# Layer 1 attention: the sixteen selection candidates of wide score tiles from four runs of eight

## The reference

```
scores = q k^T / 8, causal; key heads shared by groups of four query heads
threshold = the 64th largest score of the row
scores below the threshold = -1e30
out = softmax(scores) v, then the output projection
```

## Time and profile before

| | |
|---|---|
| median of 3 runs | 2331.82 us (2328.57 to 2334.2) |
| the profiled execution, its own time | 2331.76 us |
| its span | 2330.1 us |
| busy, share of the span | PE 81%, DVE 71%, ACT 60%, POOL 29% |
| layer 1 attention | about the last 1150 us |

### The profile page before, as it was taken

One profiled execution on the slowest core, in us unless ns is written; L12 is line 12 of the kernel. 1 busy time (PEld: TensorE's weight loads), 2 busy tenths in 40 slices (PEclk: granted clock), 3 DMA queues, 4 the chain that ended last, 5 costly groups with the idle time before them and its releaser, 6 DMA issues. The chain is left out here.

```text
span 2330.1 us, 36542 instructions
## 1 busy us (share of the span) xinstructions
PE 1883.3 (81%) x10099; PEld 1070.8 (46%) x10099; DVE 1645.3 (71%) x3759; ACT 1392.4 (60%) x2883; POOL 672.7 (29%) x1732
## 2 busy tenths in 40 slices
PE   6688888899997896888657888887888748888877
PEld 3333333357776443455424445444544424444444
DVE  4566666621113555777558998999999979999984
ACT  3255555543441331333258888988988848889874
POOL 0133333300001252000034434443444424344440
PEclk7799999999996897999978998999999979999987
DMA  6100000010001121000100100110010000000000
GB/s 189 38 17 15 17 17 14 11 37 1 0 0 45 50 87 45 0 0 0 38 20 24 28 15 29 28 28 14 28 28 19 24 14 28 18 24 28 19 19 10
DMA packets 38213, 61.99 MB, mean 27 GB/s; under 512 B 10225, under 2 KB 15347, under 8 KB 38004
## 3 DMA queue, kind: packets, MB, share of 16 engines
q1 hardware_dynamic: 38069, 60.51, 8.8%
HBM read 34.14 MB, written 17.83 MB: 22 GB/s over the span
## 5 line engine op out<-in xcount | busy, mean ns | idle before, releaser
L1568 ACT ACTIVATE a_trash<-a_sc,a_search 128x1024 bf16<-128x1024 f32 (+7 forms) x768 | 585.5, 768 | 125.2 <-POOL a_search L1515 86.9
L1311 PE MATMUL a_ps_s<-a_k,a_q 128*128 128x512 f32 (+3 forms) x768 | 332.3, 547 | 140.8 <-DVE a_sc L1710 127.1
L1344 PE MATMUL a_ps_o<-a_kT,a_v 128*65 128x512 f32 (+3 forms) x768 | 314.0, 513 | 32.4 <-ACT a_kT L1585 16.5
L1328 PE MATMUL a_ps_t<-g_ident,a_sc 128*128 128x128 f32 x1152 | 244.0, 292 | 34.6 <-ACT a_kT L1585 32.2
L1311 PEld LDWEIGHTS a_ps_s<-a_k,a_q 128*128 128x128 f32 x768 | 143.4, 209 | 257.0 <-DVE a_sc L1710 147.4
L551 DVE TENSOR_REDUCE a_top<-a_ps_row 128x1 f32<-128x512 f32 (+3 forms) x384 | 199.2, 553 | 79.0 <-PE a_ps_row L401 40.2
L530 ACT ACTIVATE a_prob<-a_ps_col 128x1024 f32<-128x1024 f32 (+7 forms) x256 | 160.4, 651 | 148.5 <-PE a_ps_col L419 147.7
L1328 PEld LDWEIGHTS a_ps_t<-g_ident,a_sc 128*128 128x128 f32 x1152 | 171.0, 148 | 123.4 <-issue 51.9
L1330 PE MATMUL a_ps_t<-a_minus,a_short 128*128 128x128 bf16 x1152 | 223.6, 227 | 0.0
L1710 DVE TENSOR_SCALAR_CACHE_REDUCE a_sc<-a_ps_s,g_search 128x1024 f32<-128x1024 f32 (+7 forms) x256 | 206.3, 806 | 23.4 <-PE a_ps_s L1313 23.2
L1684 DVE SCALAR_TENSOR_TENSOR a_below<-a_sc,a_found 128x384 f32<-128x384 f32 (+7 forms) x256 | 204.2, 819 | 1.1
(11 more groups left out here) (256 smaller groups left out, 3385.8 us busy)
## 6 DMA issues: line engine op xcount, KB each, us to landing
a_v<-g_v SPq DMA_DIRECT2D x32, 260.0 KB, 2.3
q1turned<-p_full SPq DMA_DIRECT2D x32, 256.0 KB, 2.0
a_q<-q1turned SPq DMA_DIRECT2D x32, 256.0 KB, 3.6
a_k<-k1turned SPq DMA_DIRECT2D x32, 256.0 KB, 4.0
stack<-p_parts SPq DMA_DIRECT2D x24, 256.0 KB, 3.8
a_q<-stack SPq DMA_DIRECT2D x32, 96.0 KB, 2.2
a_k<-stack SPq DMA_DIRECT2D x32, 96.0 KB, 2.2
le_w<-d_w SPq DMA_DIRECT2D x1, 2048.0 KB, 9.0
```

Of the source, the lines that this page charges most:

```text
L1311: pe.matmul(ps_s[:, j % 2, c:c + w], q[:, p, i * P:width], k[:, p, c:c + w], start=True, stop=True)
L1328: pe.matmul(out, columns(h, i)[:, c * P:(c + 1) * P], g.ident[:, :], is_transpose=True, start=True, stop=False)
L1344: m = pe.matmul(ps_o[0:VW1, lo // HALF, (lo % HALF) * P:CH], v[:, p, c, :], kT[:, u % 2, a * P:b * P], start=(c == 0), stop=(c == LAST[lo ...
L1568: act.activation(trash[:, u % 2, 0:(i + 1) * P], columns(h, i), ACT.Sign, scale=-1.0, bias=trials[:, p, c, i:i + 1], accum_out=balance[:, ...
```

## The change

Tiles 2 to 7 (384 to 1024 columns) are sorted in another way. Stage 0 splits `below` into four runs of a fourth of the width each and takes the eight largest of each, in `best`. The 32 candidates so found are sorted as before, in three more stages on 32 columns: MAX8, MATCH_REPLACE8 (into `rest`), MAX8. Tiles 0 and 1 keep the three stages.

A run may hold more than eight of the wanted values. So pick also compares the last value of each of the four runs with the threshold, sums the four comparisons in `lost` and adds it to the verdict, interleaved with the old verdict's instructions: nine instructions after thr in place of four. A head with such a row is selected again. thr gets two buffers. ScalarE's sequence stays. The orders of VectorE's and TensorE's sections are new ones: VectorE marks tiles 7 and 4 and keeps one score tile before it reads the flags, with no mark between the flags and the cutoff; TensorE multiplies the verdict before the first projection.

In the diff, a line of "..." stands for what is left out.

```diff
@@ -1145,9 +1145,10 @@
-        FIRST, FINAL = 2, 4
+        FIRST, FINAL = 7, 2
         COUNTS = 3
         NB = 16
+        QUARTERS, NARROWEST = 4, 2
         NSC = 4
         AIM = AIM1
...
         sorted_ = r.sb("sorted", [P, 2, TB, NB])
+        best = r.sb("best", [P, 2, TB, QUARTERS, 8])
+        rest = r.sb("rest", [P, TB, QUARTERS * 8])
+        last8 = r.sb("last8", [P, TB, QUARTERS])
+        lost = r.sb("lost", [P, TB])
         hit = r.sb("hit", [P, TB, NB])
         picked = r.sb("picked", [P, TB, NB])
         hits = r.sb("hits", [P, TB])
@@ -1212,7 +1217,7 @@
         verdict = r.sb("verdict", [P, TB])
         flag = r.sb("flag", [1, TB + 1], mybir.dt.int32)
         again = r.sb("again", [P, ROUNDS, 8])
-        thr = r.sb("thr", [P, TB])
+        thr = r.sb("thr", [P, 2, TB])
         cutoff = r.sb("cutoff", [P, 2, TB])
         rec = r.sb("rec", [P, TB])
@@ -1367,62 +1372,58 @@
...
-                    if leaving:
-                        project(n - 3, 0)
                     if gating:
                         pe.wait_ge(verdict_ready, n - 1)
                         pe.matmul(ps_t[0:1, odd, 0:TB], g.ones[:, 0:1], verdict[:, :], start=True, stop=True).then_inc(flag_back, 1)
                     if leaving:
+                        project(n - 3, 0)
                         project(n - 3, 1)
-                        project(n - 3, 2)
-                        project(n - 3, 3)
                     if ahead:
                         scores(n + 1, i2, p1, 2)
                     if leaving:
+                        project(n - 3, 2)
+                        project(n - 3, 3)
+                    if gating:
+                        turn(n - 2, h + 2, odd + 0, 0)
+                    if leaving:
                         project(n - 3, 4)
+                        project(n - 3, 5)
+                        project(n - 3, 6)
                     if ahead:
                         scores(n + 1, i2, p1, 3)
...
                     if gating:
                         turn(n - 2, h + 2, odd + 1, 1)
+                        weigh(*head, odd + 0, 0)
                         turn(n - 2, h + 2, odd + 2, 2)
-                        weigh(*head, odd + 0, 0)
-                        turn(n - 2, h + 2, odd + 3, 3)
                         weigh(*head, odd + 1, 1)
                     if ahead:
                         scores(n + 1, i2, p1, 5)
                     if gating:
+                        turn(n - 2, h + 2, odd + 3, 3)
                         weigh(*head, odd + 2, 2)
...
                         turn(n - 2, h + 2, odd + 8, 8)
                         weigh(*head, odd + 7, 7)
+                        weigh(*head, odd + 8, 8)
                     if late:
                         scores(n + 2, i4 * 2 + (h + 2) // 2, 1 - p1, 0)
-                    if gating:
-                        weigh(*head, odd + 8, 8)
-                    if late:
                         scores(n + 2, i4 * 2 + (h + 2) // 2, 1 - p1, 1)
@@ -1520,15 +1521,28 @@
                         pool.wait_ge(sorted_ready, n - 1)
                         after(did(pool.tensor_tensor(picked[:, :, :], hit[:, :, :], sorted_[:, p1, :, :], ALU.mult)))
                         halve(picked, some)
-                        after(did(pool.tensor_tensor(thr[:, :], some[:, :, 0], some[:, :, 1], ALU.add)))
-                        after(did(pool.tensor_scalar(bad[:, 2, :], thr[:, :], 0.0, 1.0, ALU.is_le, ALU.add)))
-                        after(did(pool.tensor_tensor(bad[:, 2, :], bad[:, 2, :], hits[:, :], ALU.subtract)))
-                        after(did(pool.tensor_tensor(bad[:, 3, :], bad[:, 2, :], limit[:, :], ALU.mult)))
-                        pool.tensor_tensor(verdict[:, :], bad[:, 3, :], bad[:, 1, :], ALU.add).then_inc(verdict_ready, 1)
+                        after(did(pool.tensor_tensor(thr[:, p, :], some[:, :, 0], some[:, :, 1], ALU.add)))
+                        cuts = thr[:, p, NARROWEST:TB].rearrange("p (s o) -> p s o", o=1).broadcast_to([P, TB - NARROWEST, QUARTERS])
+                        none = did(pool.tensor_scalar(bad[:, 2, :], thr[:, p, :], 0.0, 1.0, ALU.is_le, ALU.add))
+                        more = did(pool.tensor_tensor(last8[:, NARROWEST:TB, :], best[:, p1, NARROWEST:TB, :, 7], cuts, ALU.subtract))
+                        after(none)
+                        none = did(pool.tensor_tensor(bad[:, 2, :], bad[:, 2, :], hits[:, :], ALU.subtract))
+                        after(more)
+                        more = did(pool.tensor_scalar(last8[:, :, :], last8[:, :, :], 0.0, None, ALU.is_gt))
+                        after(none)
+                        none = did(pool.tensor_tensor(bad[:, 3, :], bad[:, 2, :], limit[:, :], ALU.mult))
+                        after(more)
+                        more = did(pool.tensor_tensor(last8[:, :, 0:2], last8[:, :, 0:2], last8[:, :, 2:4], ALU.add))
+                        after(none)
+                        did(pool.tensor_tensor(bad[:, 3, :], bad[:, 3, :], bad[:, 1, :], ALU.add))
+                        after(more)
+                        after(did(pool.tensor_tensor(lost[:, :], last8[:, :, 0], last8[:, :, 1], ALU.add)))
+                        pool.tensor_tensor(verdict[:, :], bad[:, 3, :], lost[:, :], ALU.add).then_inc(verdict_ready, 1)
 
                     pool.sem_clear(think)
                     if is_at(n, -1):
                         did(pool.memset(inverse[:, :], -1.0))
+                        did(pool.memset(last8[:, 0:NARROWEST, :], 0.0))
                         pool.wait_ge(table_in, 16 * 7)
                         after(did(pool.tensor_scalar(wide_aim[:, :], wide[:, :], AIM, None, ALU.add)))
                     if sorting:
...
-                    chain(dve.tensor_tensor(thr[:, i:i + 1], again[:, ROUNDS - 1, 7:8], top, ALU.subtract))
+                    chain(dve.tensor_tensor(thr[:, p, i:i + 1], again[:, ROUNDS - 1, 7:8], top, ALU.subtract))
...
-                        is_bad = dve.value_load(flag[0:1, i:i + 1], min_val=0, max_val=4 * P)
+                        is_bad = dve.value_load(flag[0:1, i:i + 1], min_val=0, max_val=8 * P)
@@ -1686,15 +1700,29 @@
 
                     def sort(i, stage):
 
-                        buf = lows(i)
+                        buf, stages = lows(i), 3
                         after(lane[i])
-                        if stage == 0:
+                        if i >= NARROWEST:
+                            stages = 4
+                            few = best[:, p, i, :, :].rearrange("p g e -> p (g e)")
+                        if stages == 4 and stage == 0:
+                            w = (i + 1) * P // QUARTERS
+                            for a in range(QUARTERS - 1):
+                                did(dve.max(best[:, p, i, a, :], buf[:, a * w:(a + 1) * w]))
+                            m = dve.max(best[:, p, i, QUARTERS - 1, :], buf[:, (QUARTERS - 1) * w:])
+                        elif stages == 4 and stage == 1:
+                            m = dve.max(sorted_[:, p, i, 0:8], few)
+                        elif stages == 4 and stage == 2:
+                            m = dve.match_replace(rest[:, i, :], sorted_[:, p, i, 0:8], few, -3.0e38)
+                        elif stages == 4:
+                            m = dve.max(sorted_[:, p, i, 8:16], rest[:, i, :])
+                        elif stage == 0:
                             m = dve.max(sorted_[:, p, i, 0:8], buf)
                         elif stage == 1:
                             m = dve.match_replace(buf, sorted_[:, p, i, 0:8], buf, -3.0e38)
                         else:
                             m = dve.max(sorted_[:, p, i, 8:16], buf)
-                        if i == FINAL and stage == 2:
+                        if i == FINAL and stage == stages - 1:
                             m.then_inc(sorted_ready, 1)
                         else:
                             lane[i] = did(m)
...
-                        dve.scalar_tensor_tensor(cutoff[:, p, :], thr[:, :], STEEP, ceiling[:, :],
+                        dve.scalar_tensor_tensor(cutoff[:, p, :], thr[:, p, :], STEEP, ceiling[:, :],
@@ -1756,82 +1784,83 @@
 
                     if sorting:
                         find()
-                        mark(2)
+                        mark(7)
+                        mark(4)
                     if ahead:
                         keep_scores(0)
-                    if sorting:
-                        sort(2, 0)
-                        mark(3)
-                        mark(7)
                     if gating:
                         flagged = flags()
-                    if sorting:
-                        mark(0)
-                    if gating:
                         judge(flagged)
                         after(made[0])
                         cut_off()
-                    if sorting:
-                        mark(4)
-                        sort(0, 0)
                     if ahead:
                         keep_scores(1)
+                    if sorting:
```

(71 more changed lines are left out.)

14 lines of the change are left out of this document (4 added, 10 removed).

## The result

The changed kernel takes 2339.63 us (median of 8 runs, 2337.6 to 2345.01); the kernel before, beside it on the same chip, 2331.59 (8 runs). The ratio is 1.0042, 95% interval 1.0032 to 1.0053: 8.0 us slower, where 3.5 were forecast. The profiled execution's span is 2338.7 us, 8.6 more than before.

The account below looks back on a forecast made before the run. ScalarE's sequence with the trial arithmetic was taken as the bound. 2331.76 + 11.5 (verdict) - 1.5 (small waits replaced) - 2.8 (fill) - 3.7 (drain) = 2335.3, stated as 2335 us; range for eight in ten 2322 to 2350.

Parts of the forecast that it names:

- The bound: Steady heads: ScalarE's sequence with the trial arithmetic makes the period, about 32.9 us; a faster sort cannot shorten it.
- only just fits in: VectorE in a steady head of the kernel before: its work barely fits the period of about 32.9 us.
- The sort: VectorE, tiles 2 to 7: 9.6 us removed, 3.1 added, 6.5 us a head saved; worth 0 in a steady head.
- The verdict: GpSimd, pick to cutoff: verdict ends 5.2 us after pick, ScalarE waits 0.5 us in 23 or 24 heads, +11.5 us.
- rival B: GpSimd beside marks 7 and 4: held until both end, 0.85 us a head, +12 us, 2344; chance 0.15.
- stays hidden: GpSimd's place and first_move behind pick: 0.6 us later, but the second trial is still ready in time, no cost.
- The fill: First gated head: VectorE is 6.5 us earlier, masks start at 1234.2 instead of 1237.03, -2.8 us.
- The drain: From the last search on: VectorE's work shortens by 4.6 us net, the verdict costs 0.8 more, -3.7 us.
- TensorE's order: TensorE's new order of work: costed at 0; a late turn would cost ScalarE some tenths.
- Loop ends: Five sections following a loop's end: no verdict wait counted, since ScalarE pauses 2.3 us there while pick goes on.
- The second selection: The one head that is selected again: stays as it is, 31.86 us of waiting before.
- D: A row with over eight values above the threshold in one run: head selected again, +31.9 us, 2367; chance 0.10.

Follow-up runs that it names:

- e14: The kernel before with nothing but the new sort, in the old places, without the test for a lost candidate: 2325.97 us, ratio 0.9981 to 0.9999.
- e10: e9 with the old three-pass sort over the whole width, the nine-instruction verdict comparing zeros: 2420.89 us, ratio to the kernel before 1.0377 to 1.0405.
- e1: The changed kernel with the old four-instruction verdict, without the comparison of the four runs: 2324.07 us, ratio to the kernel before 0.9967 to 0.9985.
- e9: The changed kernel with another VectorE order: marks 7, 5 and 4 moved away from pick, tile 4's sort later, nine-instruction verdict kept: 2331.79 us.
- e12: e9 with mark 3 moved from the middle of the sort to right behind mark 6, ahead of the trial arithmetic: 2317.22 us.
- e4: The changed kernel with TensorE's order of the kernel before: 2343.93 us, ratio to the kernel before 1.0042 to 1.0069.

## Why the prediction was right, and where it was off

**The bound.** Right: a VectorE relieved of 196 us (1645.3 to 1449.0 busy) gains nothing in a plain head (e14). What was too strong is "only just fits in", read as if VectorE's load no longer mattered once below the period. e10 shows that VectorE, with the old sort and an order that waits for the flags, sets 36.4 us.

**The sort.** Right: 6.5 us a head were forecast. Between the last search and the last pick VectorE is busy 19.37 us, 25.81 before: 6.44 less. The instructions on 32 columns, the size that no row showed, last 0.176 to 0.185 us each (192 of each form); in the chain-free middle of a head they follow each other at about 0.1. Each form, by line:

```profile
L1716 DVE MATCH_REPLACE8 a_rest<-a_sorted,a_best 128x32 f32<-128x32 f32 x192 | 33.4, 176 | 0.0
L1714 DVE MAX8 a_sorted<-a_best 128x8 f32<-128x32 f32 x192 | 32.4, 182 | 0.0
```

By the Trainium skill, VectorE: DVE Perf Modes, section on the TRN2 errata, with its fixed term of about 150 cycles, the estimate was a saving of 4.5 us; the measured 6.44 goes against it for instructions that follow each other.

**The verdict.** thr 3.02 us after pick (3.0 forecast), thr to verdict 2.13 (2.2), pick to verdict 5.15 (5.2), flags and cutoff +0.28 and +0.91 (0.29, 0.90). That is the forecast's chain, step by step. GpSimd does get in between marks 7 and 4, as forecast; rival B's order, by which it would wait for both, doesn't occur. The time alone would not have told the forecast from B, as 2339.6 is as far from 2335 as from 2344. The wait reads 0.68 in 11 heads of the loop, 0.2 to 0.6 in the others and 0.3 in the written-out ones at the end. Taken together, 23 steady heads wait 51.8 - 32.4 - 5.0 - 2.2 - 0.2 = 12.0 us (less the selection, the first head and the last two), where 11.5 were forecast. e1 shows its price from the other side: without the five more instructions 15.6 us less.

**The written-out sections.** This is the step that was off. "Queued behind pick on GpSimd are place and first_move ... stays hidden" looked at the second trial alone. The third trial's arithmetic, which ScalarE waits for in every head, was taken to be untouched by VectorE's new order. Now, in five heads (four at the end, one at the start), mark 3 lies on a short step of it, L1510 in four of them and L1500 in the last, 0.5 to 0.6 us each: +2.8. In three heads of the loop (masks at 1303.62, 1778.01 and 2047.77) it starts 16.4 us after the masks and stretches L1514 from 0.20 to 0.38 to 0.40 us: +0.6. Of the 13.6 us that the steady heads lose, 10.0 were forecast (11.5 less 1.5); the waits for the cutoff bring 0.5 more, and mark 3 brings 3.4. These make 13.9, but not an exact account: the five heads behind a loop's end, put at 0, are together 1.3 us shorter than before, so that about 1 us is not assigned. The prediction had the mechanism for the pick and did not ask where the other marks would fall. e9 and e12 show that this hold is worth 13 to 15 us in another order, as much as the five more instructions (e1).

**The fill** gave 2.2 us, 2.8 were forecast.

**The drain** gave 2.9 instead of 3.7. VectorE and GpSimd behind the last search:

```profile
2282.62 0.15 DVE L1745 TENSOR_REDUCE a_flag<-a_ps_t 1x1 int32<-1x8 f32 x1 [2.91 <-PE a_ps_t L1377]
2283.64 0.17 DVE L1758 SCALAR_TENSOR_TENSOR a_cutoff<-a_thr,a_ceiling 128x8 f32<-128x8 f32 x1 [0.87 <-DVE a_flag L1745]
2288.48 0.18 DVE L1766 RECIPROCAL a_rec<-a_ps_o 128x3 f32<-128x3 f32 x1 [1.70 <-DVEq L1682]
2302.58 0.46 POOL L1522 TENSOR_TENSOR a_picked<-a_hit,a_sorted 128x128 f32<-128x128 f32 x1 [16.59 <-DVE a_sorted L1718]
```

Search to pick is 25.3 us, 3.0 less than before, not 4.6: VectorE's work fell as forecast, but its idle time rose by 3.5 us and not 1.9. The idle time before the flags (2.91) and behind them (0.87) is 1.7 us more than before, about what the sum had; it left out the 1.70 behind the cutoff, ahead of the read of TensorE's projection (a_ps_o), whose clock is at 0.50 there. Pick to masks costs 0.7 more (0.8 forecast), and from the masks to the end it is 0.6 less, which was not forecast.

**TensorE's order** at 0: not refuted (e4's interval overlaps that of the changed kernel); by its medians and its first masks the new order may gain some 3 us. **Loop ends** covered by the 2.3 us pause: right; the masks there start with no wait. **The second selection** stays, 32.43 us in one head. **A lost row** (D) does not occur.

**The sum**: 3.6 more in the steady heads, 0.6 less at the fill, 0.8 less at the drain are the 5.1 us (rounded) between 8.6 and 3.5. By the medians it is 8.0: slower by more than 0.2%, where the forecast lay just inside it.

## What to carry to other kernels

Relieving an engine that isn't the bound gives idle time. That can be spent on an order of work with better places in it, and here the order decided the sign: the same instructions take 2339.6 or 2317.2 us. When two engines exclude each other, list every long instruction of the one against every short chain of the other that somebody waits for, in all sections, and put the long ones beside waits or beside one long instruction of the other engine. And where one order has late and punctual heads, compare the granted clock of the two before blaming the order.
